# Softmax normalization before the value matmul, by transposes, in a windowed attention and gated FFN kernel

## What is computed

```
x: (1, 16384, 1024), 16 heads of 64, one shared K and V head, windows of 256
q = x @ q_w.T;  k, v = split(x @ kv_w.T)
attn = softmax(q_window @ k_window.T / 8)
out = (attn @ v_window) @ proj_w.T + proj_b
x = layernorm(x + out)
gate = x @ wg.T;  up = x @ wu.T          (int8 weights / 127, 3072 wide)
x = layernorm(x + (silu(gate) * up) @ wd.T)
```

## Time and profile before

| what | value |
|---|---|
| median of 2 runs | 982.07 us (979.81 to 984.33) |
| profiled execution, its own time | 977.16 us |
| its span, first to last instruction, slowest core | 975.4 us |
| spans of the eight cores | 968.6 to 975.4 us |
| mean granted TensorE clock of the cores | 0.889 to 0.896 of full |
| TensorE busy | 797.8 us (82%) |
| VectorE busy | 307.9 us (32%) |
| ScalarE busy | 195.1 us (20%) |

### The profile page before, as it was taken

How to read it: one execution, slowest core, us unless ns; L and a number is a source line. 1 busy time by engine, 2 the same in 40 slices (tenths; PEclk the granted TensorE clock), 3 DMA queues, 4 the chain that set the end, 5 groups by cost and what they waited for, 6 DMA issues and landing times.

```text
span 975.4 us, 11104 instructions; the slowest of 8 cores (968.6 to 975.4 us)
## 1 busy us (share of the span) xinstructions
PE 797.8 (82%) x3872; PEld 331.2 (34%) x3872; DVE 307.9 (32%) x410; ACT 195.1 (20%) x361; POOL 124.8 (13%) x247
## 2 busy tenths in 40 slices
PE   3657777758989999958888888676798999999996
PEld 3112222223434444412333333222343444443332
DVE  0136676432222211112444454642222221111111
ACT  0032332222121111102222222321212111111111
POOL 4000010001212233300000010000122223310000
PEclk8567776888999999968998999789899999999999
DMA  8960120224434455461111131122443445531221
GB/s 103 243 177 12 23 54 1 80 85 149 141 113 138 134 153 152 111 111 44 44 44 44 44 87 33 44 66 97 143 142 115 141 141 151 151 98 41 73 70 65
DMA packets 47173, 94.05 MB, mean 96 GB/s; under 512 B 5776, under 2 KB 5776, under 8 KB 47120
## 3 DMA queue, kind: packets, MB, share of 16 engines
q0 software_dynamic: 37744, 67.91, 27.5%
q1 hardware_dynamic: 9376, 25.43, 8.0%
HBM read 63.44 MB, written 12.58 MB: 78 GB/s over the span
## 4 chain that ended last, share of the span: by engine, by line
PE 59%; DVE 16%; DMA 12%; issue 6%; ACT 4%; POOL 1%; DVEq 0%; SPq 0%; ACTq 0%; POOLq 0%
PE ps L265 59%; DVE pool L369 8%; DMA wqsb<-wq 6%; DMA x<-xtm 4%; ACT r L700 2%; DVE r L692 2%; DVE silu L692 2%; DVE pool L387 2%; DMA xbf<-xfm 2%; ACT silu L700 1%; DVE pool L321 1%; DVE x2s L710 1%; DVE xbf L434 1%; DVE hbuf L574 1%; DMA wuw<-wu 0%
## 5 line engine op out<-in xcount | busy, mean ns | idle before, releaser
L265 PE MATMUL ps<-xbf,wgw 128*128 128x512 bf16 x768 | 185.9, 386 | 14.9 <-DVE xbf L434 14.9
L265 PE MATMUL ps<-xbf,wuw 128*128 128x512 bf16 x768 | 187.3, 388 | 11.2 <-DVE hbuf L574 11.1
L265 PE MATMUL ps<-wdres,hbuf 128*128 128x512 bf16 x768 | 188.1, 391 | 7.6 <-PE ps L265 1.0
L574 DVE SCALAR_TENSOR_TENSOR hbuf<-ps,silu 128x512 bf16<-128x512 f32 x96 | 66.4, 692 | 270.5 <-PE ps L265 266.1
L369 DVE RECIPROCAL pool<-ps 128x256 f32<-128x256 f32 x64 | 112.5, 1757 | 32.5 <-PE ps L265 29.1
L265 PEld LDWEIGHTS ps<-xbf,wgw 128*128 128x128 bf16 x768 | 75.6, 99 | 109.7 <-issue 24.4
L569 ACT ACTIVATE silu<-ps 128x512 f32<-128x512 f32 x96 | 56.9, 597 | 278.1 <-PE ps L265 278.1
L265 PEld LDWEIGHTS ps<-xbf,wuw 128*128 128x128 bf16 x768 | 76.1, 100 | 106.9 <-issue 20.6
L265 PEld LDWEIGHTS ps<-wdres,hbuf 128*128 128x128 bf16 x768 | 70.9, 99 | 115.2 <-issue 46.6
L350 ACT ACTIVATE pool<-ps 128x512 bf16<-128x512 f32 x128 | 74.6, 595 | 157.3 <-PE ps L265 147.7
L544 POOL DMA_DIRECT2D wgw<-wg x96 | 50.8, 529 | 343.4 <-PE ps L265 343.4
(11 more groups left out here) (51 smaller groups left out, 264.4 us busy)
## 6 DMA issues: line engine op xcount, KB each, us to landing
wgw<-wg POOLq DMA_DIRECT2D x96, 256.0 KB, 2.6
wuw<-wu POOLq DMA_DIRECT2D x96, 256.0 KB, 2.6
x<-xtm SPq DMA_DIRECT2D x16, 512.0 KB, 3.7
y<-x SPq DMA_DIRECT2D x16, 512.0 KB, 2.9
wdres<-wd POOLq DMA_DIRECT2D x1, 6144.0 KB, 50.2
wqsb<-wq POOLq DMA_DIRECT2D x18, 256.0 KB, 4.9
xbf<-xfm POOLq DMA_DIRECT2D x16, 256.0 KB, 13.2
x2scr<-x2s SPq DMA_DIRECT2D x16, 256.0 KB, 2.2
```

Of the source, the lines that this page charges most:

```text
L265: last = t.matmul(o, l, r, start=st_, stop=sp, tile_position=tpos)
L574: return v.scalar_tensor_tensor(H_sb[:, m, n * 512:(n + 1) * 512], bank(6)[:, 0:512], FS, silu_sb[:, par, n * 512:(n + 1) * 512], ALU.mult ...
```

## The change

The scores are computed with queries on the partitions and keys along the columns. The exponentials are taken in four pieces of 256 columns, each with its row sum as accumulated output (`accum_out`), in two slots instead of five. A new step, `emit_norm`, takes the reciprocal of 128x4 sums and multiplies the 128x1024 exponentials by it. `emit_AT` turns the normalized weights around by eight 128x128 transposes into bank 7 and copies them to SBUF. AV uses that copy, and its result is copied to O with no factor. The ones matrix goes. Stage `i` issues S(i), norm(i-1), transposes(i-2), AV(i-3); the drain has three stages, and the first one comes after the first projection and the start of its layer norm. The setup and the 80 matmuls are listed after the first loads.

```diff
-        E3_v = pap[:, 10240:15360].rearrange("p (e x) -> p e x", e=5)
-        rr_v = pap[:, 15360:16384].bitcast(F32).rearrange(
-            "p (a w) -> p a w", a=2)
-        ones64_v = sb("ones64", [128, 64], BF16)[:, :]
+        E_v = pap[:, 10240:12288].rearrange("p (a h t u) -> p a h t u", a=2, h=2, t=2)
+        A_v = pap[:, 12288:14336].rearrange("p (a h t u) -> p a h t u", a=2, h=2, t=2)
+        AT_v = pap[:, 14336:16384].rearrange("p (a h c w) -> p a h c w", a=2, h=2, c=2)
...
-        def setup_fn(g):
...
-        P.op("t", warm_fn, reads=("ident",), writes=("pb0",), note="warmup")
         P.dma("gd", "wkv", lambda g: g.dma_start(
...
             writes=("wdres",), note="ld wd")
+        def setup_fn(g):
...
+        P.op("t", warm_fn, reads=("ident",), writes=("pb0",), note="warmup")
...
         def emit_S(st, j, b, bm):
...
-                for uh in range(2):
-                    lhsT = krep_v[h * 64:(h + 1) * 64,
-                                  b * 256 + uh * 128: b * 256 + (uh + 1) * 128]
-                    rhs = Q_v[h * 64:(h + 1) * 64, j % 2, b * 256:(b + 1) * 256]
+                for wt in range(2):
+                    lhsT = Q_v[h * 64:(h + 1) * 64, j % 2,
+                               b * 256 + wt * 128: b * 256 + (wt + 1) * 128]
+                    rhs = krep_v[h * 64:(h + 1) * 64, b * 256:(b + 1) * 256]
...
-                    return s.activation(
-                        E3_v[:, e3, h * 512:(h + 1) * 512],
-                        bank(bk)[:, 0:512], AF.Exp, bias=-CSHIFT)
+                for wt in range(2):
+                    def exp_fn(s, bk=bk, wt=wt, h=h, par=par):
+                        return s.activation(
+                            E_v[:, par, h, wt, :],
+                            bank(bk)[:, wt * 256:(wt + 1) * 256],
+                            AF.Exp, bias=-CSHIFT,
+                            accum_out=sums_sb[:, par, 2 * h + wt: 2 * h + wt + 1])
+                    P.op("c", exp_fn, reads=(f"pb{bk}", "consts"),
+                         writes=(f"E{par}", f"sums{par}"),
...
+        def emit_norm(j, b):
             par = b % 2
...
             P.op("v", lambda v, par=par: v.reciprocal(
-                rr_v[:, par, :], bank(7)[:, par * 256:(par + 1) * 256]),
+                rr_sb[:, par, :], sums_sb[:, par, :]),
...
+            def norm_fn(v, par=par):
+                rb = rr_sb[:, par, :].unsqueeze(2).broadcast_to([128, 4, 256])
+                return v.scalar_tensor_tensor(
+                    A_v[:, par, :, :, :].rearrange("p a b u -> p (a b) u"),
+                    E_v[:, par, :, :, :].rearrange("p a b u -> p (a b) u"),
+                    1.0, rb, ALU.mult, ALU.mult)
...
+        def emit_AT(j, b):
...
+                            last = t.transpose(
+                                bankB(7)[:, off:off + 128],
+                                A_v[:, par, h, wt, c * 128:(c + 1) * 128],
+                                identB[:, :])
...
+                return v.tensor_copy(
+                    AT_v[:, par, :, :, :],
+                    bankB(7)[:, 0:1024].rearrange("p (h c w) -> p h c w", h=2, c=2))
...
         def emit_AV(j, b):
...
-                return v.scalar_tensor_tensor(
+                return v.tensor_copy(
                     O_v[:, j, b * 256:(b + 1) * 256],
-                    bank(4)[:, par * 256:(par + 1) * 256], 1.0,
-                    rr_v[:, par, :], ALU.mult, ALU.mult)
+                    bank(4)[:, par * 256:(par + 1) * 256])
...
         def emit_projseg(st, drain=()):
+            emit_proj_mm(st, 0)
+            fin0 = emit_proj_lnspill(st, 0, 0, scratch="silu", defer=True)
             if drain:
                 drain[0]()
-            emit_proj_mm(st, 0)
-            fin0 = emit_proj_lnspill(st, 0, 0, scratch="silu", defer=True)
-            if len(drain) > 1:
-                drain[1]()
             fin0()
             emit_proj_mm(st, 1)
             fin1 = emit_proj_lnspill(st, 1, 1, scratch="silu", defer=True)
-            if len(drain) > 2:
-                drain[2]()
+            if len(drain) > 1:
+                drain[1]()
             fin1()
-            for f in drain[3:]:
+            for f in drain[2:]:
                 f()
```

More of the change, by code:

```diff
@@ L259, in build_program, with warm_fn @@
             writes=("wdres",), note="ld wd")
+        def setup_fn(g):
+            for i, cv in enumerate(CONSTS):
+                g.memset(cpool[:, i:i + 1], float(cv))
+            g.memset(ones_sb[:, :], 1.0)
+            g.memset(identB[:, :], 0.0)
+            g.memset(identB2[:, :], 0.0)
+            g.drain()
+            g.affine_select(out=identB[:, :], in_=identB[:, :],
+                            compare_op=ALU.not_equal, fill=1.0, base=0,
+                            pattern=[[-1, 128]], channel_multiplier=1)
+            g.affine_select(out=identB2[:, :], in_=identB2[:, :],
+                            compare_op=ALU.not_equal, fill=1.0, base=-64,
+                            pattern=[[-1, 64]], channel_multiplier=1)
+            g.drain()
+            return g.nop()
+        P.op("g", setup_fn, writes=("consts", "ident"), note="setup")
+        def warm_fn(t):
+            last = None
+            for _ in range(80):
+                last = t.matmul(bank(0)[:, 0:128], identB[:, :],
+                                identB[:, :], start=True, stop=True)
+            return last
+        P.op("t", warm_fn, reads=("ident",), writes=("pb0",), note="warmup")
         def mm_group(pairs, note, reads, writes):
@@ L334, in emit_S @@
             par = b % 2
-            e3 = (j * NBLK + b) % 5
             for h in range(2):
@@ L338, in emit_S @@
                 pairs = []
[L339 to L343 removed]
+                for wt in range(2):
+                    lhsT = Q_v[h * 64:(h + 1) * 64, j % 2,
+                               b * 256 + wt * 128: b * 256 + (wt + 1) * 128]
+                    rhs = krep_v[h * 64:(h + 1) * 64, b * 256:(b + 1) * 256]
+                    pairs.append((bank(bk)[:, wt * 256:(wt + 1) * 256],
                                   lhsT, rhs, True, True, None))
@@ new lines, in emit_norm @@
+        def emit_norm(j, b):
+            par = b % 2
+            P.op("v", lambda v, par=par: v.reciprocal(
+                rr_sb[:, par, :], sums_sb[:, par, :]),
+                reads=(f"sums{par}",), writes=(f"rr{par}",),
+                note=f"recip j{j} b{b}")
+            def norm_fn(v, par=par):
[4 more added lines that the diff above has]
+                    1.0, rb, ALU.mult, ALU.mult)
+            P.op("v", norm_fn, reads=(f"E{par}", f"rr{par}"), writes=(f"A{par}",),
+                 note=f"norm j{j} b{b}")
@@ new lines, in emit_AT, with at_fn, atev_fn @@
+        def emit_AT(j, b):
+            par = b % 2
+            def at_fn(t, par=par):
+                last = None
+                for h in range(2):
+                    for c in range(2):
+                        for wt in range(2):
+                            off = h * 512 + c * 256 + wt * 128
+                            last = t.transpose(
+                                bankB(7)[:, off:off + 128],
+                                A_v[:, par, h, wt, c * 128:(c + 1) * 128],
+                                identB[:, :])
+                return last
+            P.op("t", at_fn, reads=(f"A{par}", "ident"), writes=("pb7",),
+                 note=f"AT j{j} b{b}")
+            def atev_fn(v, par=par):
+                return v.tensor_copy(
+                    AT_v[:, par, :, :, :],
+                    bankB(7)[:, 0:1024].rearrange("p (h c w) -> p h c w", h=2, c=2))
+            P.op("v", atev_fn, reads=("pb7",), writes=(f"AT{par}",),
+                 note=f"ATevac j{j} b{b}")
@@ L397, in chain_stages @@
             out = []
-            for i in range(NCH + 4):
+            for i in range(NCH + 3):
                 def stage(i=i, st=st, bm=bm):
@@ L655, in build_program @@
         stages0 = chain_stages(0, BM_SOLO)
-        for f in stages0[:-4]:
+        for f in stages0[:-3]:
             f()
-        drain = stages0[-4:]
+        drain = stages0[-3:]
         for st in range(NST):
```

48 lines of the change are left out of this document (18 added, 30 removed).

## The result

The changed kernel is slower: 1013.77 us median of 11 runs (1008.59 to 1015.36), against 980.12 us for the kernel before in the same comparison. The ratio is 1.0326, 95% interval 1.0299 to 1.0352. The forecast was 981.5 us with a range of 963 to 1010.

What follows compares the result with a forecast made beforehand. TensorE was taken to wait for VectorE's reciprocal and ScalarE's exponentials in both attention passes. -2.1 + 0 - 1.0 - 0.7 + 3.2 = -0.6 us, so 981.5 us beside the 982.07 median; range 963 to 1010.

Steps and rivals of the forecast that it cites:

- The setup moved behind the loads: Start of the kernel: DMA issues begin earlier, wq j1's second load lands earlier; -2.1 us, bounds -2.5 and +0.5.
- VectorE and ScalarE per block: Softmax work per window and head pair: VectorE 2.55 us, 0.4 more than before; ScalarE 2.3 against some 1.3.
- TensorE: Per block, eight transposes replace four matmuls against ones: 0.46 against 0.32 us, 0.14 more, showing only in the second pass.
- First pass: Attention with nothing beside it: 13.7 us per head pair against 13.78, no change, bounds 0.5 both ways per pair.
- rival C: Faster: fewer idle pieces keep TensorE's clock up, first Q half at full clock; 23.5 us gained, 958 us; chance 0.10.
- The drain stages: End of first pass: first projection 2.0 us earlier, later load of x costs 1.0; sum -1.0 us.
- The -0.7 for the second pass: The drain's gain in the second pass, put at -0.7 us beside -1.0 in the first.
- Second pass: Attention woven between down-projection units: Q waits -6.3, transposes +4.5, after layer norms +2.1, clock +2.9; sum +3.2 us.
- two extra falls of the clock: Second pass: TensorE waits longer in one piece behind the layer norm, two more falls at 1.44 us, +2.9.
- A (the clock): Slower: transposes and waits gathered behind the layer norm drop TensorE's clock in each cycle; 31 us, 1010 us; chance 0.20.
- B (ScalarE the bound): Slower: half-width exponentials still cost 0.595, 3.7 us per block on ScalarE; +31, 1013 us; chance 0.07.
- D (no gain at the start): Start: the load of wq j1 doesn't move, so the start gains nothing; 983.6 us; chance 0.08.

Runs made afterwards that it cites:

- e2: Kernel before with only the setup and warm-up moved behind the first loads, old softmax: 1012.59 us, ratio 1.0332.
- e9: Kernel before with the setup moved behind the loads and its two GpSimd drains replaced by semaphore waits, old softmax: 978.06 us, ratio 0.9986.
- e3: Changed kernel, setup still behind the loads, its two GpSimd drains replaced by semaphore waits: 975.52 us, ratio 0.9956 to the kernel before.
- e1: Changed kernel with setup and warm-up back ahead of all loads, softmax rewrite kept: 977.56 us, ratio 0.9981 to the kernel before.
- e6: e3 without the second load of wq's tile 1: 971.68 us, ratio 0.9907 to the kernel before.
- e5: e1 with the three drain stages placed as in the kernel before: 976.65 us, ratio 0.9963 to the kernel before.
- e7: e3 with the drain stages placed as in e5 and without the second load of wq's tile 1: 971.71 us, ratio 0.9910 to the kernel before.
- e8: Kernel before, setup in front, with one more GpSimd drain behind the DMA issues: 983.8 and 986.5 us, against 980.9.
- e4: Changed kernel with its drains, but the big loads wp and wd issued behind the setup: 983.65 us, ratio 1.0036 to the kernel before.
- e10: Kernel before with 160 transposes as warm-up in place of the 80 matmuls: 980.57 us, one execution.
- e11: Kernel before with 160 warm-up matmuls instead of 80: 979.48 us, one execution.

## Why the prediction was wrong

**The setup moved behind the loads: the step that failed.** It counted the DMA issues that the setup was moved past (9 us of GpSimd's queue) and not what the setup itself does there: its `g.drain()` waits for the loads that GpSimd issued. The forecast was -2.1 us with bounds of -2.5 and +0.5, and "setup and the 80 warm-up matmuls run about 9 us later, while the first chunks are still in flight". Measured, the warm-up ran 54.7 us later (57.46 against the old start at 2.72), and where the sum has -2.1 the drains cost 34.5 us in the old kernel (e2, e9). What the step says of the issues is open: without the drains the medians gain some 2 us, within the noise. In e9's trace Q of the second pair starts at 59.98 against 62.07, the 2.1 earlier of the forecast; in e3's it starts at 61.64 against 61.12 in e1, no earlier, so e3's 2.0 did not come from there. In the trace of before the drain between memset and affine_select had no load ahead of it and showed as 0.2 us, so its price there said nothing of the price behind 8 MB of loads; no rival had it, and the range, whose bounds came from durations of work, could not hold it.

**VectorE and ScalarE per block: right. TensorE: too low.** Every price of VectorE and ScalarE came within 0.03 us (the groups above), ScalarE's spacing too: in the changed kernel four exponentials of a block started at 106.83, 107.40, 108.02 and 108.59, 0.57 to 0.62 apart against 0.58. Eight transposes took 0.55 us to the next start (145.22 to 145.77 in e1), where I had 0.46; against the 0.32 of the four ones-matmuls that is 0.23 more per block in place of 0.14, and 7.4 us in place of 4.5 over the 32 blocks of the second pass.

**First pass: right in its sum, with a higher clock than assumed.** 13.45 us a pair in e1 against 13.7. The granted clock rose, though:

```profile
62.00:159.00 97.00, 73.81 (x575) 33.85 (x573) 75.35 (x130) 53.51 (x232) 4.76 (x9) 0.85 0.14 26
443.00:615.00 172.00, 148.60 (x880) 64.69 (x877) 86.42 (x150) 66.66 (x257) 5.28 (x10) 0.94 0.19 48
```

0.85 in place of 0.73 over the first pass. The clock of rival C came, but not the gain that it priced: the first Q half, which C had at full clock, still took 3.28 us (141.67 in e1, 3.33 before). The clock was higher ahead of it, 1.00 and 0.83 over the two stretches from the scores at 135.51 on, where the earlier trace rows has 0.92 and 0.50, and there TensorE is not what ends last: the scores at 135.51 and 148.96 above both follow 0.95 us of idle time that VectorE ended.

**The drain stages: half right.** The first projection started at the forecast time (10.2 against 10.1), so the gain of 2.0 was there. From there to the third projection 18.5 was forecast; it took 21.1 in e1, 20.6 in the changed kernel, 19.3 in e3 and 18.2 in e6, so the loss was anything from 0.6 to 3.5 in place of 1.0. The load of x is part of that spread: in e1 it took 5.3 us there (171.40 to 176.67), where I had taken over 3.7. By e5, e6 and e7 little of either reaches the end, since SyncE's queue sets the pace of the projections. The -0.7 for the second pass had no working of its own, and no run measures it.

**Second pass: its sum can't be told from the forecast, its parts were off.** +3.2 was forecast. From the first down matmul to the first projection of super-tile 1, e1 took 627.9 - 406.0 = 221.9, against 629.5 - 407.8 = 221.7 before: +0.2. But six traces with the old softmax have 218.4 to 223.3 us for this stretch, 220.7 in the mean, and seven with the new one 220.8 to 225.3, 222.2 in the mean. So the rewrite costs 1.5 us there, give or take some 2. The waits of TensorE in this pass, before and then in e1:

```profile
PE ps L265 <- DVE pool L369: 17.3, 22, 1.7
```

```profile
PE ps L265 <- ACT pool L350: 13.6, 14, 3.8
...
PE ps L382 <- DVE pool L390: 3.0, 6, 0.5
```

Q no longer waits for bank 7, as the step said. The step counted only Q's 6.3 us of the 17.3 that TensorE waited for the reciprocal; of the whole, 6.6 are left in e1 (3.0 for the transposes' copy, 3.6 in one piece for the small reciprocal), and the wait for ScalarE grew from 10.0 to 13.6. All of its waits there together went from 36.0 us to 26.6, and against that stand the dearer transposes. What did not come are the two extra falls of the clock: 0.94 from 443 to 615 us in e1, and before:

```profile
443.00:617.00 174.00, 142.95 (x776) 57.06 (x776) 81.34 (x97) 46.54 (x89) 5.29 (x10) 0.94 0.17 47
```

**Rivals.** A (the clock) and B (ScalarE the bound) are out: in e1 the clock is not lower, and the exponentials cost 383 ns, not 595. The time fell next to what they had priced, 1010 and 1013, for another reason; being near a rival's number says nothing for its mechanism. D (no gain at the start) was the nearest in subject: it asked only whether the move gains, not what it could block. Whether it is right in that stays open, since e9's trace speaks against it and e3's for it.

## What to carry to other kernels

Before moving a block of instructions behind DMA issues on GpSimd, look for a drain in it: here it waited until the loads issued ahead had landed, and a semaphore between the two instructions did the same ordering in 0.2 us. Price a moved barrier by what will be in flight at its new place, never by its duration at the old one; in the page it shows as "issue" on an engine that does nothing, and as one long wait of the engine behind it. When a stage is paced by one queue (here SyncE's spill and load), a wait removed elsewhere in it is cover and returns little.

## What the runs showed of the hardware

A drain on GpSimd ended when the last load issued ahead of it by GpSimd had landed. GpSimd's next instruction came at 56.7 us with wd's load landed near 55.9 (the changed kernel), at 58.3 with 57.5 (e2), at 62.9 with 61.6 (e8), and at 27.3 with 26.6 for the small loads alone (e4). GpSimd's memset and affine_select run at once with the same loads in flight if no drain stands between, 0.20 us apart (e3). Transposes bring TensorE's clock up much as matmuls do, 160 of them in 10.88 us against 10.34 (e10, e11, one execution each). And in the first pass the granted clock rose from 0.73 to 0.85 with eight transposes per block in place of four matmuls, at nearly the same time per pair (13.45 us against 13.78).
